# Weight transposes and scale rows of a quantised feed-forward moved from TensorE to DMA transposes and a DRAM round trip, with new instruction orders

## The chip, the cores and the metric

The kernel runs on one core of one Trainium2 chip. The metric is the device time of one execution in microseconds (us). Three runs of the kernel before stand beside each other with their median, and one more execution was taken with the profiler; all rows below are of that one. The engines are TensorE (PE; its weight loads are PEld), VectorE (DVE), ScalarE (ACT), GpSimd (POOL) and SyncE (SP), which here only issues transfers.

## The reference

One decoder layer on 8 sequences of 128 tokens with 256 features:

```
x = x + self_attention(layernorm(x))        # 16 query heads, 4 key heads, RoPE, causal, biases
x = x + cross_attention(layernorm(x), ctx)  # one head of 256, keys = values = ctx, masked
x = x + ffn(layernorm(x))
ffn: xq = quant(x); w1q = quant(w_gate_up)  # per row: scale = max|v| / 127, q = clip(round(v / scale)) * scale
     gate, up = split(xq @ w1q.T)           # 2 x 704 columns
     h = silu(gate) * up
     return quant(h) @ quant(w_down).T      # w_down is 256 x 704
```

`w_gate_up` is 1408 x 256, 11 tiles of 128 rows; its rows 704 to 1407 are the up half, that is half of tile 5 and tiles 6 to 10. Both weights come with their output rows on the partitions, so they have to be transposed before they can be multiplied, and they are quantised on the chip in each execution.

## The kernel before

Each sequence is one tile of 128 tokens. For each of the eight the kernel goes through the same steps, named by functions with the sequence's index: `project`, `rotate`, `rotate_c`, `rotate_sum`, `transpose_qk`, `evacuate_qk`, `scores`, `max_scores`, `transpose_q_max`, `score_keys`, `exp_self`, `drop_later_keys`, `weigh_values`, `normalise_y`, `project_out`, `residual_1` for self-attention; `transpose_x1`, `cross_scores`, `exp_cross`, `transpose_cross_p`, `readout`, `residual_2` for cross-attention; `quantise_x`, `transpose_x_int`, `gate_product`, `up_product`, `hidden`, `quantise_h`, `transpose_h`, `down`, `scale_down`, `add_residual` for the feed-forward.

No scheduler runs on the chip. Each engine has its own stream of instructions, and the order in it is written out by hand at the end of the engine's block (L546 to L578 for PE, L744 to L765 ACT, L1035 to L1063 DVE, L1190 to L1203 POOL). The streams meet through semaphores: `done(engine, name, j)` waits for the j-th signal. An instruction that waits holds up all that stand behind it on its engine. The sequences are interleaved, so that PE works on one while the other engines work on the next ones.

PSUM's banks tie the orders together. `ps_s` (four banks) holds the scores, and in the feed-forward the gate and up products; `gate_product(0)` therefore waits until the last `exp_self` is done. `ps_q` holds projections and their transposes, `ps_y` the attention output and later `down`, `ps_x` the cross-attention. `ps_r` is the one for everything else: the warm-up matmuls `keep_warm` (L262, matmuls of zeros at the start), `mean_ctx` (L280), `readout`, `transpose_x_int`, and all transposes of the weights. Each user of `ps_r` names the signal it has to wait for, the evacuation of the user before it.

The weights go this way. SP loads W1 in three parts and W2 in one, and the context last (L241 to L244). DVE takes the absolute maxima, the scales and their inverses; ACT writes integers, `quantise_w1(0..4)` (L638) into `w1_int`, `quantise_w2` into `w2_int`, both int16. The gate half is rescaled on POOL, transposed by PE in f32 and split into a high and a low part. The up half stays integer: PE transposes it as 16-bit data in two steps (`transpose_up`, L399, 6 transposes each), ACT evacuates it to `up_int` (`evacuate_up`, L656). Its scales, one per output column, are spread over all partitions by `spread_up_scale` (L410, 3 f32 matmuls each, which the trace shows as 6) and evacuated to `up_row` (L666); POOL multiplies the gate by that row (`widen_gate`, L1147). W2 is transposed in two halves (`transpose_w2`, L420, 6 transposes and the spread of its scale), and DVE evacuates it to `w2_T` and `w2_row` (`evacuate_w2`, L953), which `down` and `scale_down` use.

SP's queue issues the loads at the start and then waits for each output tile and stores it (L245 to L251).

Of the kernel before, what the change touches and what calls it, by code (L numbers as in the profile page):

```python
# [32 lines left out]
def decoder_layer(nc, w_first_in, x_zero_in, x_first_in, x_second_in, wo_in, mask_in, x_in, xT_in, ctxT_in, ctx_in, w1_in, w2_in, out):  # L33
# [15 lines left out]
    GT = -(-FF // P)  # L49
# [7 lines left out]
    with ExitStack() as stack:  # L57
# [46 lines left out]
        w2_row = sb("w2_row", [P, D])  # L104
# [60 lines left out]

        def x_token(j):
            return x_second[:, 0:D] if j == 1 else x_aug[:, j, 0:D]

        def x_feature(j, c):
# [30 lines left out]
            up_transposed up_int_ready up_scale_spread up_row_ready  # L200
            w2_amax_done w2_scale_done w2_inv_ready w2_int_ready w2_transposed w2_ready
# [32 lines left out]
        def _(sp):  # L234
# [10 lines left out]
            for j in range(B):  # L245
                if j < B - 1:
# [3 lines left out]
                sp.dma_start(out[j], y_out[:, j, :]).then_inc(s["out_stored"], 16)  # L250
            sp.wait_ge(s["out_stored"], 16 * B)  # L251
# [3 lines left out]
        def _(pe):  # L255
# [143 lines left out]
            def transpose_up(p, last, k):  # L399

                bank_r_free(pe, last, k)
                done(pe, "w1_int_ready", 3 + p)
                done(pe, "ident_b_ready", 0)
                for i, o in enumerate(range(5 + 3 * p, 8 + 3 * p)):
                    for c in range(DC):
                        last = nc.tensor.transpose(ps16(ps_r)[:, (2 * i + c) * P:(2 * i + c + 1) * P],
                                                   w1_int[:, o, c * P:(c + 1) * P].bitcast(BF16), ident_b[:, :])
                last.then_inc(s["up_transposed"], 1)

            def spread_up_scale(p, last, k):  # L410
# [850 lines left out]
```

## Time and profile before

| | |
|---|---|
| three runs | 102.81, 101.42, 103.0 us; median 102.81 |
| profiled execution | 101.47 us, of which the span of instructions is 99.8 |
| granted TensorE clock over the span | 0.987 of full |
| PE, PEld busy | 90.2 us (90%), 68.8 (69%) |
| DVE, ACT, POOL busy | 75.7, 65.7, 66.1 us |
| chain that ended last | PE 72%, DVE 10%, POOL 7%, issue 5%, ACT 3% |
| DMA | 8.34 MB, nearly all of it in the first 23 us |

The profile is of one execution. Busy time is per engine over the span of 99.8 us; matmuls are pipelined, and their ends are modelled, so busy times of neighbouring groups overlap by a little. The chain of waits is followed back from the last instruction, at each step to what released it or to the instruction before it on its engine; its durations don't overlap. The 1.7 us between span and execution time are start and end around the instructions.

### The profile page before, as it was taken

The numbers are of one execution on the slowest core, as the hardware profiler recorded it, in microseconds if no ns is written. First come the engines' busy times: TensorE is split into PE (matmuls) and PEld (weight loads), VectorE is DVE, ScalarE is ACT, GpSimd is POOL, SyncE is SP. The second block draws the span as 40 slices with busy tenths as digits, with TensorE's granted clock in tenths as the row PEclk, the third lists the DMA queues.
The fourth block names the chain that finished last, engine by engine and source line by source line (L and its number), as shares of the span: only waits on it lengthen the run. The fifth ranks groups of instructions, "written<-read, shape, count | busy, mean of one in ns | idle before, by whom it ended". The sixth has DMA issues, their size and how long they took to land.

```text
span 99.8 us, 2432 instructions
## 1 busy us (share of the span) xinstructions
PE 90.2 (90%) x804; PEld 68.8 (69%) x804; DVE 75.7 (76%) x217; ACT 65.7 (66%) x175; POOL 66.1 (66%) x136
## 2 busy tenths in 40 slices
PE   5999699999889999989999999979999999999560
PEld 4698467977576676767776777768778887775220
DVE  5046979957998988877896659797977788988731
ACT  1404216938839886776597878969986996988410
POOL 6266847975787977914638788848868962892220
PEclk9999999999999999999999999999999999999995
DMA  2999999940000000000000000000000010012121
GB/s 36 346 337 415 419 407 409 360 143 3 3 0 7 0 3 0 7 0 0 0 7 0 0 0 0 3 7 0 0 0 0 0 56 7 0 59 99 55 103 53
DMA packets 4521, 8.34 MB, mean 84 GB/s; under 512 B 349, under 2 KB 3358, under 8 KB 4382
## 3 DMA queue, kind: packets, MB, share of 16 engines
q1 hardware_dynamic: 4272, 7.96, 21.7%
q10 hardware_dynamic: 238, 0.23, 0.9%
q8 instruction: 6, 0.10, 0.4%
q14 instruction: 5, 0.04, 0.1%
HBM read 7.15 MB, written 1.05 MB: 82 GB/s over the span
## 4 chain that ended last, share of the span: by engine, by line
PE 72%; DVE 10%; POOL 7%; issue 5%; ACT 3%; DVEq 0%; POOLq 0%; ACTq 0%
PE ps_s L443 14%; PE ps_r L262 6%; PE ps_q L303 6%; PE ps_y L525 4%; PE ps_r L289 4%; PE ps_r L386 3%; PE ps_x L375 3%; PE ps_s L339 3%; PE ps_y L351 3%; PE ps_y L359 3%; PE ps_q L311 2%; PE ps_x L365 2%; DVE rot L846 2%; PE ps_s L469 2%; PE ps_y L354 2%
## 5 line engine op out<-in xcount | busy, mean ns | idle before, releaser
L1156 POOL TENSOR_TENSOR gate_up<-gate,up_row 128x704 f32<-128x704 f32 x7 | 11.9, 1698 | 3.7 <-ACT gate L723 3.5
L262 PE MATMUL ps_r<-warm 128*128 128x256 bf16 x60 | 9.4, 317 | 1.1 <-DVE warm L771 1.1
L262 PEld LDWEIGHTS ps_r<-warm 128*128 128x128 bf16 x60 | 6.7, 115 | 3.0 <-DVE warm L771 1.1
L1125 POOL TENSOR_TENSOR rot_c<-rot,b_rope 128x128 f32<-128x128 f32 x8 | 3.7, 459 | 7.5 <-DVE rot L846 7.5
L869 DVE RECIPROCAL y_rsum<-ps_y 128x128 f32<-128x128 f32 x8 | 7.6, 951 | 1.1 <-PE ps_y L354 1.0
L443 PE MATMUL ps_s<-gate_hi,x_int_T 128*128 128x352 f32 x28 | 7.5, 350 | 0.0
L1187 POOL TENSOR_TENSOR y_out<-ffn,x_aug 128x256 f32<-128x256 f32 x7 | 5.1, 729 | 3.7 <-DVE ffn L1025 3.7
L525 PE MATMUL ps_y<-w_T,h_T 128*128 128x256 bf16 (+1 forms) x42 | 6.5, 276 | 0.9 <-DVE ffn L1025 0.8
L443 PE MATMUL ps_s<-up_int,x_int_T 128*128 128x352 f32 x32 | 6.9, 337 | 0.0
L443 PE MATMUL ps_s<-gate_lo,x_int_T 128*128 128x352 f32 x28 | 6.8, 323 | 0.0
L610 ACT ACTIVATE p_self_T<-ps_s 128x512 f32<-128x512 f32 x8 | 4.8, 597 | 2.4 <-PE ps_s L339 2.4
L734 ACT ACTIVATE h_int<-hid,h_inv 128x704 int16<-128x704 f32 x7 | 6.1, 878 | 0.3 <-DVE h_inv L1020 0.2
L1006 DVE SCALAR_TENSOR_TENSOR hid<-ps_s,x_scale,gate_up 128x704 f32<-128x704 f32 x5 | 4.8, 951 | 1.9 <-PE ps_s L443 1.3
L1011 DVE TENSOR_REDUCE h_amax<-hid 128x1 f32<-128x704 f32 x7 | 6.1, 872 | 0.0
L525 PEld LDWEIGHTS ps_y<-w_T,h_T 128*128 128x128 bf16 (+1 forms) x42 | 3.5, 97 | 3.5 <-issue 1.5
L864 DVE TENSOR_REDUCE qk_rot<-ps_s 128x4 f32<-128x512 f32 x8 | 5.4, 678 | 0.5 <-PE ps_s L327 0.4
L723 ACT ACTIVATE gate<-ps_s,x_scale 128x704 f32<-128x704 f32 x5 | 4.2, 847 | 2.3 <-PE ps_s L443 2.3
L846 DVE TENSOR_TENSOR rot<-ps_q,rope_r 128x256 f32<-128x256 f32 x8 | 3.4, 423 | 2.9 <-PE ps_q L303 2.9
L1025 DVE SCALAR_TENSOR_TENSOR ffn<-ps_y,h_scale,w_row 128x256 f32<-128x256 f32 x8 | 3.8, 480 | 2.2 <-PE ps_y L525 1.3
L303 PE MATMUL ps_q<-wqkv_c,xT 128*128 128x192 f32 x24 | 5.4, 346 | 0.0
L375 PE MATMUL ps_x<-ctxT,x1c_T 128*128 128x128 f32 x32 | 5.3, 288 | 0.0
L386 PE MATMUL ps_r<-ctx_aug,p_cross_T 128*128 128x257 f32 x16 | 5.2, 406 | 0.0
(194 smaller groups left out, 285.8 us busy)
## 6 DMA issues: line engine op xcount, KB each, us to landing
ctxT<-in_ctxT SPq DMA_DIRECT2D x1, 1024.0 KB, 8.6
w_raw<-in_w SPq DMA_DIRECT2D x2, 512.0 KB, 11.0
ctx_aug<-in_ctx SPq DMA_DIRECT2D x1, 1024.0 KB, 17.0
out_x<-y_out SPq DMA_DIRECT2D x8, 128.0 KB, 1.7
x_aug<-in_x SPq DMA_DIRECT2D x1, 768.0 KB, 6.8
xT<-in_xT SPq DMA_DIRECT2D x1, 768.0 KB, 9.8
w_raw<-in_w SPq DMA_DIRECT2D x1, 704.0 KB, 14.6
x_first<-in_x_first SPq DMA_DIRECT2D x1, 416.0 KB, 4.3
```

The source lines that it names most:

```text
L262: nc.tensor.matmul(ps_r[:, 0:2 * T], warm[:, 0:P], warm[:, :], start=True, stop=True)
L303: last = nc.tensor.matmul(ps_q[:, 0:6 * QK], x_feature(j, c), wqkv_c[:, c, :, :], start=c == 0, stop=c == DC - 1)
L375: last = nc.tensor.matmul(ps_c, x1c_T[j % 3][:, c, :], ctxT[:, j, c, :], start=False, stop=c == DC - 1)
L386: nc.tensor.matmul(ps_r[:, 0:DA], p_cross_T[:, j, :], ctx_aug[:, j, :], start=True, stop=True).then_inc(s["readout_done"], 1)
L443: last = nc.tensor.matmul(ps_s[:, first + i, 0:FH], x_int_T[:, j, c, :], w[:, c, i * FH:(i + 1) * FH], start=c == 0 and w is parts[0], sto ...
L525: last = nc.tensor.matmul(ps_y[:, 0:D], h_T[j % 2][0:n, f, :], w2_T[0:n, f, :], start=f == 0, stop=f == FC - 1)
L734: nc.scalar.mul(h_int[j % 2][:, :], hid[j % 2][:, :, :].rearrange("p i f -> p (i f)"), h_inv[:, j:j + 1]).then_inc(s["h_int_ready"], 1)
L846: nc.vector.tensor_tensor(rot[j % 3][:, :, :].rearrange("p (m t) n -> p m (t n)", m=2), ps_q[:, 0:4 * QK].unsqueeze(1).to_broadcast([P, 2, ...
L864: nc.vector.tensor_reduce(qk_rot[j % 3][:, 0, :, DH], ps_s[:, :, 0:T], AX.X, ALU.max, negate=True).then_inc(s["negmax_done"], 1)
L869: nc.vector.reciprocal(y_rsum[j % 3][:, :], ps_ys).then_inc(s["y_rsum_done"], 1)
L1011: nc.vector.tensor_reduce(h_amax[:, j:j + 1], hid[j % 2][:, :, :].rearrange("p i f -> p (i f)"), AX.X, ALU.max, apply_absolute_value=True) ...
L1156: nc.gpsimd.tensor_tensor(gate_up[j % 2][:, :, :], gate[j % 2][:, :, :], up_row[:, :].rearrange("p (i f) -> p i f", i=2), ALU.mult).then_i ...
```

## The change

The up half of W1 and all of W2 are no longer transposed by PE. SP issues a transposing transfer from SBUF to SBUF: one for the six up tiles (twelve blocks of 128 x 128 16-bit values) as soon as `quantise_w1(4)` is done, into a region of `w1_raw`, which is free by then; and two for W2 (six blocks each), after DVE has written W2's integers as bf16 into another region of `w1_raw` padded to 768 columns (`widen_w2`). ACT then only casts the up half (`evacuate_up`, now by halves of the contraction, from SBUF). W2's transfers write `w2_T` directly.

All 13 columns of scales (11 of W1, 2 of W2) are in one tile `w_scale`. One small transpose on PE turns it into 13 rows, ACT copies them (`copy_scales`), SP stores them to DRAM, waits for that store, and loads 960 values back, broadcast to 128 partitions (`out_rows`), which takes the place of `up_row` and `w2_row`. `scale_down` and the first `widen_gate` wait for that load.

The gate half goes the way it did. The orders of all four engines are new; in the diff their parts around the moved work stand. Of removed functions only the first line is shown, since they are printed above.

```diff
-GT = -(-FF // P)
+GT = FF // P
...
-w1_scale = sb("w1_scale", [P, WT])
+w_scale = sb("w_scale", [P, WT + DC])
-w1_q = sb("w1_q", [P, GT, D])
+w1_q = sb("w1_q", [P, GT + 1, D])
-up_row = sb("up_row", [P, FF])
+scale_rows = sb("scale_rows", [WT + DC, P])
+out_rows = sb("out_rows", [P, FF + D])
-w2_scale = sb("w2_scale", [P, DC])
-w2_row = sb("w2_row", [P, D])
...
+w1_flat = w1_raw[:, :, :].rearrange("p o d -> p (o d)")
+UT = (WT - GT) * DC * P // 2
+up_T = w1_flat[:, 0:UT].bitcast(I16).rearrange("p (o c t) -> p o c t", c=DC, t=P)
+padded = w1_flat[:, UT:UT + 2 * FC * P].bitcast(BF16).rearrange("p (i f) -> p i f", f=FC * P)
+w2_bf = padded[:, 0:DC]
+h_bf = [padded[:, DC + i] for i in range(2)]
+w1_scale = w_scale[:, 0:WT]
+w2_scale = w_scale[:, WT:WT + DC]
+up_row = out_rows[:, 0:FF]
+w2_row = out_rows[:, FF:FF + D]
+scale_rows_dram = nc.dram_tensor("scale_rows_dram", [WT + DC, P], F32).ap()
...
+    done(sp, "w1_int_ready", 4)
+    sp.dma_start_transpose(up_T[:, :, :, :].rearrange("p o c t -> p (o c) t"),
+                           w1_int[:, GT:WT, :].rearrange("p o d -> p (o d)")).then_inc(s["up_T_loaded"], 16)
+    done(sp, "scale_rows_ready", 0)
+    sp.dma_start(scale_rows_dram, scale_rows[:, :]).then_inc(s["scale_rows_stored"], 16)
+    sp.wait_ge(s["scale_rows_stored"], 16)
+    sp.dma_start(out_rows[:, :], scale_rows_dram.rearrange("o p -> (o p)")[FF:2 * FF + D].unsqueeze(0).to_broadcast([P, FF + D])).then_inc(s["rows_loaded"], 16)
+    done(sp, "pads_zero", 0)
+    for c in range(DC):
+        done(sp, "w2_bf_ready", c)
+        sp.dma_start_transpose(w2_T[:, :, c * P:(c + 1) * P], w2_bf[:, c, :]).then_inc(s[f"w2_T_{c}_loaded"], 16)
+
+    def store_out(j):
+
+        if j < LAST:
             done(sp, "y_out_ready", j)
         else:
             done(sp, "last_y_out_ready", 0)
         sp.dma_start(out[j], y_out[:, j, :]).then_inc(s["out_stored"], 16)
...
-    def transpose_up(p, last, k):
...
-    def spread_up_scale(p, last, k):
...
+    def transpose_scales(last, k):
 
         bank_r_free(pe, last, k)
         done(pe, "w1_scale_done", 2)
+        done(pe, "w2_scale_done", 0)
         done(pe, "ident_ready", 0)
-        for i, o in enumerate(range(5 + 3 * p, 8 + 3 * p)):
...
+        nc.tensor.transpose(ps_r[0:WT + DC, 0:P], w_scale[:, :], ident[:, :]).then_inc(s["scales_transposed"], 1)
...
-            done(pe, "w2_ready", DC - 1)
+            for c in range(DC):
+                pe.wait_ge(s[f"w2_T_{c}_loaded"], 16)
...
-    keep_warm(30); mean_w_first(); keep_warm(6); bias_wo(); keep_warm(4); project(0); keep_warm(11)
-    transpose_qk(0); mask_scores(0); project(1); scores(0); keep_warm(7); transpose_q_max(0)
-    keep_warm(2); score_keys(0); transpose_qk(1); mean_ctx(None, 0); project(2); weigh_values(0)
-    mask_scores(1); transpose_gate(0, "valid_ready", 0); scores(1); transpose_qk(2); project_out(0)
...
-    transpose_up(0, "x_int_T_ready", 2); score_keys(7); project_out(6); cross_scores(5); gate_product(0)
-    readout(4, "up_int_ready", 0); transpose_cross_p(5); weigh_values(7); transpose_x1(6)
-    readout(5, "x2_ready", 4); cross_scores(6); transpose_up(1, "x2_ready", 5); gate_product(1)
-    up_product(0); transpose_cross_p(6); transpose_x_int(3, "up_int_ready", 1); project_out(7)
-    transpose_x1(7); up_product(1); transpose_x_int(4, "x_int_T_ready", 3); cross_scores(7)
-    readout(6, "x_int_T_ready", 4); gate_product(2); transpose_w2(0, "x2_ready", 6)
...
+    keep_warm(30); mean_w_first(); keep_warm(6); bias_wo(); keep_warm(2); mask_scores(0); project(0)
+    keep_warm(11); transpose_qk(0); scores(0); project(1); keep_warm(5); transpose_q_max(0)
+    keep_warm(4); score_keys(0); transpose_qk(1); keep_warm(3); mask_scores(1); scores(1); project(2)
+    weigh_values(0); transpose_q_max(1); mean_ctx(None, 0); score_keys(1); transpose_qk(2)
+    transpose_gate(0, "valid_ready", 0); project_out(0); project(3); mask_scores(2); scores(2)
+    transpose_x1(0); weigh_values(1); transpose_gate(1, "gate_lo_ready", 0); transpose_q_max(2)
+    transpose_qk(3); cross_scores(0); score_keys(2); project(4); project_out(1); transpose_cross_p(0)
+    transpose_gate(2, "gate_lo_ready", 1); mask_scores(3); transpose_x1(1); scores(3); transpose_qk(4)
+    weigh_values(2); transpose_scales("gate_lo_ready", 2); transpose_q_max(3); cross_scores(1)
+    score_keys(3); readout(0, "scale_rows_ready", 0); project(5); mask_scores(4); project_out(2)
...
+    cross_scores(5); project_out(6); gate_product(0); weigh_values(7); transpose_cross_p(5)
+    up_product(0); transpose_x1(6); readout(5, "x2_ready", 4); cross_scores(6); project_out(7)
+    transpose_x_int(3, "x2_ready", 5); gate_product(1); transpose_cross_p(6)
+    transpose_x_int(4, "x_int_T_ready", 3); transpose_x1(7); up_product(1); cross_scores(7)
+    readout(6, "x_int_T_ready", 4); gate_product(2); transpose_cross_p(7); readout(7, "x2_ready", 6)
+    transpose_h(0); up_product(2); transpose_x_int(5, "x2_ready", 7); gate_product(3)
...
-    def evacuate_up(p):
...
-    def evacuate_up_scale(p):
...
+    def evacuate_up(c):
+
+        act.wait_ge(s["up_T_loaded"], 16)
+        nc.scalar.copy(up_int[:, c, 0:FL], up_T[:, 0, c, FL:P])
+        nc.scalar.copy(up_int[:, c, FL:FF].rearrange("p (o t) -> p o t", t=P), up_T[:, 1:WT - GT, c, :]).then_inc(s["up_int_ready"], 1)
+
+    def copy_scales():
+
+        done(act, "scales_transposed", 0)
+        nc.scalar.copy(scale_rows[:, :], ps_r[0:WT + DC, 0:P]).then_inc(s["scale_rows_ready"], 1)
...
+    copy_key_bias(); centre_wo(); scale_v(0); evacuate_qk(0); evacuate_q_max(0); scale_v(1); exp_self(0)
+    evacuate_qk(1); quantise_w1(0); scale_v(2); quantise_w1(1); evacuate_q_max(1); quantise_w1(2)
+    quantise_w1(3); quantise_w1(4); evacuate_qk(2); exp_self(1); upper_gate(0); quantise_w2(0)
+    scale_v(3); square_1(0); quantise_w2(1); evacuate_x1(0); evacuate_q_max(2); evacuate_qk(3)
+    upper_gate(1); exp_cross(0); exp_self(2); evacuate_cross_p(0); upper_gate(2); scale_v(4)
+    square_1(1); evacuate_qk(4); evacuate_x1(1); copy_scales(); evacuate_q_max(3); evacuate_up(0)
+    exp_self(3); exp_cross(1); evacuate_up(1); evacuate_cross_p(1); square_2(0); scale_v(5); square_1(2)
...
-    def evacuate_w2(c):
...
+    def widen_w2(c):
+
+        if c == 0:
+            done(dve, "w1_int_ready", 4)
+            nc.vector.memset(padded[:, :, FF:], 0.0).then_inc(s["pads_zero"], 1)
+        done(dve, "w2_int_ready", c)
+        nc.vector.tensor_copy(w2_bf[:, c, 0:FF], w2_int[:, c, :]).then_inc(s["w2_bf_ready"], 1)
...
         done(dve, "down_done", j)
-        nc.vector.scalar_tensor_tensor(ffn[j % 3][:, :], ps_y[:, 0:D], h_scale[:, j:j + 1], w2_row[:, :],
+        dve.wait_ge(s["rows_loaded"], 16)
+        nc.vector.scalar_tensor_tensor(ffn[j % 3][:, :], ps_y[:, 0:D], h_scale[:, j:j + 1], w2_row,
                                        ALU.mult, ALU.mult).then_inc(s["ffn_ready"], 1)
...
+    stats_1(0); aggregate_1(0, 1); sum_wq(); copy_ident(); centre_w_first(); stats_1(1)
+    aggregate_1(1, 2); find_valid(); rotate(0); stats_1(2); rotate_sum(0); stats_1(3); exclude()
+    stats_1(4); stats_1(5); max_scores(0); rotate(1); stats_1(6); stats_1(7); rotate_sum(1)
+    aggregate_1(2, B); amax_w1(0); scale_w1(0); invert_w1(0); max_scores(1); rotate(2)
+    amax_w1(1); scale_w1(1); invert_w1(1); rotate_sum(2); amax_w1(2); scale_w1(2); invert_w1(2)
+    invert_sums(0); normalise_y(0); keep_valid(); amax_w2(); scale_w2(); invert_w2(); residual_1(0)
+    rotate(3); lower_gate(0); max_scores(2); rotate_sum(3); invert_sums(1); widen_w2(0)
+    negate_ctx_mean(); max_cross(0); normalise_y(1); bias_cross(0); lower_gate(1); rotate(4)
+    residual_1(1); invert_cross_sum(0); rotate_sum(4); lower_gate(2); max_scores(3); invert_sums(2)
...
+    step_x(4); invert_x(4); invert_sums(7); finish_gate(0); normalise_y(7); residual_2(5); max_cross(6)
+    amax_x(5); bias_cross(6); residual_1(7); hidden(0); amax_h(0); step_x(5); invert_x(5)
+    scale_h(0); invert_h(0); finish_gate(1); max_cross(7); invert_cross_sum(6); bias_cross(7)
+    residual_2(6); amax_x(6); invert_cross_sum(7); hidden(1); residual_2(7); step_x(6); invert_x(6)
...
-            done(pool, "up_row_ready", 1)
+            pool.wait_ge(s["rows_loaded"], 16)
...
+    rstd_1(0, 1, 1); scale_rope(0); sum_bias(); rope_bias(); rotate_c(0); rstd_1(1, 2, 2); centre_x(0)
+    scale_rope(1); rotate_c(1); centre_x(1); rstd_1(2, B, 3); drop_later_keys(0); scale_rope(2)
+    centre_x(2); scale_rope(3); rotate_c(2); centre_x(3); rescale_gate(0); scale_rope(4)
+    rescale_gate(1); scale_rope(5); centre_x(4); centre_x(5); rescale_gate(2); drop_later_keys(1)
...
```

## Rows read from the trace of the kernel before

**Rows 1.** The page: busy time and instructions by engine; granted clock in 40 slices.
```profile
PE 90.2 (90%) x804; PEld 68.8 (69%) x804; DVE 75.7 (76%) x217; ACT 65.7 (66%) x175; POOL 66.1 (66%) x136
...
PEclk9999999999999999999999999999999999999995
```

**Rows 2.** Table by stretches: width, busy us of PE, PEld, DVE, ACT, POOL; clock, DMA.
```profile
16.50:30.00 13.50, 12.68 (x135) 10.28 (x135) 11.53 (x27) 9.14 (x26) 10.97 (x23) 1.00 0.35 124
...
30.00:40.00 10.00, 9.71 (x113) 6.84 (x113) 8.96 (x26) 8.23 (x27) 7.99 (x20) 1.00 0.01 2
...
65.00:75.00 10.00, 9.41 (x68) 7.81 (x69) 8.65 (x26) 8.38 (x19) 7.29 (x12) 1.00 0.01 2
```

**Rows 3.** Chain that ended last: start, us on the chain, what.
```profile
47.75 0.67 PE ps_r L416 x6
...
49.42 0.26 PE ps_x L380
...
55.34 0.51 PE ps_r L406 x6
...
61.60 0.36 PE ps_r L406 x6
...
69.05 0.47 PE ps_r L426 x6
69.52 0.43 PE ps_r L428 x2
...
70.84 0.63 PE ps_r L426 x6
```

**Rows 4.** Timeline of PE, 65 to 71 us: start, us, line, idle before.
```profile
65.43 0.41 PE L365 MATMUL ps_x<-ident,x1c 128*128 128x128 f32 x2 [0.76 <-DVE x1c L879]
...
70.84 0.63 PE L426 MATMUL ps_r<-ident_b,w_int 128*128 128x128 bf16 x6 [0.16 <-DVE w_row L958]
```

**Rows 5.** Groups by line and shape: count, busy us, mean ns.
```profile
L956 DVE CAST w_T<-ps_r 128x640 bf16<-128x640 int16 x2 | 1.0, 492 | 0.3 <-PE ps_r L428 0.3
...
L957 DVE CAST w_T<-ps_r 64x128 bf16<-64x128 int16 x2 | 0.4, 206 | 0.0
...
L958 DVE COPY w_row<-ps_r 128x128 f32<-128x128 f32 x2 | 0.5, 273 | 0.0
...
L672 ACT COPY up_row<-ps_r 128x384 f32<-128x384 f32 x1 | 0.5, 468 | 0.0
...
L664 ACT CAST up_int<-ps_r 128x768 fp32r<-128x768 int16 x1 | 0.8, 802 | 0.1
...
L703 ACT CAST h_T<-ps_x 128x640 bf16<-128x640 int16 x4 | 2.7, 685 | 0.6 <-PE ps_x L492 0.5
...
L704 ACT CAST h_T<-ps_x 64x128 bf16<-64x128 int16 x4 | 1.0, 258 | 0.0
```

**Rows 6.** Timelines of POOL and PE around 16 us.
```profile
15.75 1.34 POOL L1089 TENSOR_TENSOR r<-ln_var,pow_exp 128x6 f32<-128x6 f32 x1
...
18.09 0.64 POOL L1130 TENSOR_SCALAR_AFFINE_SELECT p_self_T<-p_self_T 128x512 f32<-128x512 f32 x1
...
16.43 3.78 PE L289 MATMUL ps_r<-mean_w,ctxT 128*128 128x60 f32 x32
```

**Rows 7.** Timeline of ACT: last W1 quantisation; fourth query-maximum evacuation.
```profile
23.54 1.31 ACT L642 ACTIVATE w_int<-w_raw,w_inv 128x256 int16<-128x256 f32 x3
...
33.66 0.27 ACT L605 COPY q_max_T<-ps_s 128x128 f32<-128x128 f32 x1
```

**Rows 8.** The page: GB/s by slice, the two queues, the output stores.
```profile
GB/s 36 346 337 415 419 407 409 360 143 3 3 0 7 0 3 0 7 0 0 0 7 0 0 0 0 3 7 0 0 0 0 0 56 7 0 59 99 55 103 53
...
q1 hardware_dynamic: 4272, 7.96, 21.7%
q10 hardware_dynamic: 238, 0.23, 0.9%
...
out_x<-y_out SPq DMA_DIRECT2D x8, 128.0 KB, 1.7
```

More of the change, by code:

```diff
@@ L552, in _ @@
-            transpose_x1(0); transpose_qk(3); mask_scores(2); scores(2); weigh_values(1); project(4)
-            transpose_q_max(2); cross_scores(0); score_keys(2); transpose_gate(2, "gate_lo_ready", 1)
-            project_out(1); mask_scores(3); scores(3); transpose_cross_p(0); weigh_values(2); transpose_x1(1)
-            transpose_q_max(3); transpose_qk(4); readout(0, "gate_lo_ready", 2); score_keys(3); project(5)
-            cross_scores(1); mask_scores(4); project_out(2); scores(4); transpose_qk(5); transpose_cross_p(1)
@@ L557, in _ @@
-            weigh_values(3); transpose_q_max(4); readout(1, "x2_ready", 0); transpose_x1(2); score_keys(4)
-            project(6); cross_scores(2); mask_scores(5); transpose_x_int(0, "x2_ready", 1); project_out(3)
-            scores(5); transpose_qk(6); transpose_cross_p(2); transpose_x_int(1, "x_int_T_ready", 0)
-            weigh_values(4); transpose_q_max(5); project(7); transpose_x1(3); score_keys(5)
-            readout(2, "x_int_T_ready", 1); cross_scores(3); mask_scores(6); project_out(4)
@@ new lines, in _ @@
+            weigh_values(2); transpose_scales("gate_lo_ready", 2); transpose_q_max(3); cross_scores(1)
+            score_keys(3); readout(0, "scale_rows_ready", 0); project(5); mask_scores(4); project_out(2)
+            transpose_cross_p(1); scores(4); transpose_x1(2); weigh_values(3); readout(1, "x2_ready", 0)
+            transpose_q_max(4); transpose_qk(5); cross_scores(2); score_keys(4)
+            transpose_x_int(0, "x2_ready", 1); project_out(3); project(6); mask_scores(5); transpose_cross_p(2)
@@ new lines, in _ @@
+            scores(5); transpose_x1(3); weigh_values(4); transpose_q_max(5); readout(2, "x_int_T_ready", 0)
+            transpose_qk(6); score_keys(5); cross_scores(3); transpose_x_int(1, "x2_ready", 2); project(7)
+            project_out(4); mask_scores(6); transpose_cross_p(3); scores(6); weigh_values(5); transpose_x1(4)
+            transpose_q_max(6); transpose_qk(7); readout(3, "x_int_T_ready", 1); score_keys(6); cross_scores(4)
+            project_out(5); mask_scores(7); transpose_x_int(2, "x2_ready", 3); scores(7); transpose_cross_p(4)
@@ L581, in _ @@
+            transpose_h(4); last_gate(0); down(3); last_gate(1); up_product(7); transpose_h(5); down(4)
+            transpose_h(6); down(5); down(6); last_transpose_h_a(); last_transpose_h_b(); last_down_a()
+            last_down_b()
         @block.scalar
```

170 lines of the change are left out of this document (53 added, 117 removed).

## The prediction

> **What bounds the kernel now.** I read the page's busy times first. TensorE (PE) is busy 90.2 of 99.8 us, the other three between 65 and 76, and the granted clock is full in every slice but the last [rows 1]; so neither the clock nor a single slow stage is to be looked for, and the question is whether PE's own work is the path. The table by stretches says so: from 30 to 40 us PE is busy 9.71 of 10 us, as much in the ten that follow, and from 65 to 75 it is 9.4, while VectorE (DVE) has 8.96 in the first of these stretches and ScalarE (ACT) 8.2 [rows 2]. The chain of waits then goes from PE group to PE group through the whole middle, and among its pieces stand all the transposes and spreads that the change takes away, each with the time that it holds on the chain [rows 3]. PE's timeline shows where it does stand still late in the kernel: 0.76 us before `transpose_x1(7)`, for a residual of DVE, and 0.16 us between the two W2 transposes [rows 4].
>
> **Taken from PE.** Two `spread_up_scale` at 0.67 us each, two `transpose_up` at 0.51 and 0.36, and for W2 0.47 and 0.63 for the transposes and twice 0.43 for the spread of its scale (of each pair of spreads one stands) [rows 3]: 1.34 + 0.87 + 1.96 = 4.17 us. The 0.16 us wait between the W2 halves goes too, because nothing of W2 passes through the shared bank `ps_r` any more [rows 4]: 4.33.
>
> **Added to PE.** One f32 transpose of 13 columns. The nearest row is a whole 128-column f32 transpose with 0.26 us of chain [rows 3]; it can't cost more, and not less than nothing. I take 0.2. The count of warm-up matmuls goes from 60 to 61, all ahead of the 16 us mark, where PE waits anyway: nothing. What hides it is the wait for loads and rotations; uncovered it would be one matmul of that kind.
>
> **DVE.** `evacuate_w2` goes: per half 0.49 + 0.21 + 0.27 us [rows 5], 1.94 in all, at 70 to 73 us, when PE has other work; worth nothing beyond the 0.16 counted. `widen_w2` comes: two int16 to bf16 copies of 704 columns and a memset of 4 x 64 columns. The nearest copy is 640 columns out of PSUM in 0.49 [rows 5]; from SBUF it may be twice as fast, so a copy costs 0.27 to 0.54 and both with the memset 0.6 to 1.3; I take 1.0, nearer the row. They fall between about 28 and 36 us, where DVE has only 1.04 us in 10 free [rows 2]. About a third should show: 0.3.
>
> **ACT.** Removed: the scale rows (0.47 for the larger, about 0.4 for its pair) and the up evacuations (0.80 for the second, and about as much for the first, of 640 columns in two pieces) [rows 5], about 2.5 us. Added: per half of up a cast of 640 columns and one of 64, by the h casts 0.69 and 0.26 [rows 5], so 1.9, and the 0.26 copy of the scales. The sum hardly changes, but 1.9 us move from 57 to 63 us to about 34 to 38 us, in front of `exp_self(3)` and `exp_cross(1)`. The two W2 quantisations leave that stretch for the one before, where ACT is busy 9.1 of 13.5 us [rows 2]; that is the cover. With four small fillers taken out of PE's order as well, some handover in between that was hidden by them is now seen. None of it has a row; bounds are 0 and the 1.9 us, and as the loops through the banks are much shorter than the five us per sequence, I take 0.4.
>
> **The start.** `scores(0)` now comes before `project(1)`, which brings the first sequence forward, and `mean_ctx` comes after `weigh_values(0)` and `transpose_q_max(1)`. `mean_ctx` used to cover a wait: its 3.78 us ran from 16.43 us on while GpSimd (POOL) took 1.34 us for the power of six columns from 15.75 us and masked the probabilities only at 18.09 [rows 6]. Now the mask follows the power directly, 17.1 + 0.64 = 17.7 us. PE gets there after `scores(1)` and `project(2)` at about 17.1, so it idles some 0.6 us, then does the same work as before. Against that, scores and rotation are further on. Counting the same set of PE pieces done, I come to a loss between 0.1 and 0.7 and take 0.2.
>
> **The late gap.** In the new order `normalise_y(7)` and `project_out(7)` stand ahead of `hidden(0)`'s work, so the 0.76 us before `transpose_x1(7)` may go wholly or not at all; I take 0.4.
>
> **SP's queue and the transfers.** What is queued behind SP's new waits: the row store and load, the two W2 transposes, and only then the output stores. The first store is due near 79 us, so none of them is held up unless the whole queue is some 40 us late. Of the new transfers three have much room: the scale rows are needed by `widen_gate(0)` at 60 us and written near 34, and a 128 KB output store lands 1.7 us after its issue [rows 8], so store and a broadcast of 492 KB are over near 39; the W2 transposes are needed by `down(0)` near 73. They cost nothing.
>
> The up transpose is the one that can hurt. `quantise_w1(4)` runs from 23.5 to 24.9 us now and moves forward, so 24.9 is the latest issue; `evacuate_up(0)` stands directly behind `evacuate_q_max(3)`, which now runs at 33.66 [rows 7]. The room is 9.0 us, and behind the waiting ACT instruction stand `exp_self(3)` and everything after it, so each us beyond goes straight onto the end. No row shows a transposing transfer. Lower bound: its 393 KB at the 410 GB/s of the load phase are 1.0 us, with the 1.7 of landing 2.7. As 1,536 pieces of 256 bytes, by the ACT queue's packets (0.9% of 16 x 99.8 us over 238 packets, 60 ns each) 1,536 x 60 / 16 = 5.8 us, with landing 7.5; by the SP queue's mean of 81 ns 9.5 [rows 8]. Upper bound: twelve blocks of 128 x 128 one after the other, each at a whole small transfer's 1.7 us, 20.4. I take 7.5, since small packets are the nearest row: in time, by 1.5 us, cost 0.
>
> Two pages of the Trainium skill disagree on this transfer. "DMA: Bandwidth & Descriptors", section "Latency and other measured facts", has a DMA transpose at 261 GB/s with a broken middle dimension; by that the up half would take an estimated 1.5 us and the sum stays. "VectorE: DVE Perf Modes", section "The three transpose paths", gives 1309 ns for one 128 x 128 block and advises TensorE for it; twelve in a row would be an estimated 15.7 us, 6.7 late, and the kernel would be near 104.6 us. No row here tells which holds.
>
> **Sum.** -4.33 + 0.2 + 0.3 + 0.4 + 0.2 - 0.4 = -3.6 us. The profiled execution took 101.47 us for its span of 99.8, so it would become 97.9, with a span near 96.2. The median of the three runs, 102.81, is 1.3 above the profiled one; from there the same gain leads to 99.2. I take 98.6, between the two.
>
> **Rivals.**
> A, the forecast: PE stays the bound and the removed work is gained. For it: the chain pieces [rows 3] and the full stretches [rows 2]. Its own range is 96.6 to 100.4. Chance 0.64.
> B, the removed pieces were fillers. DVE at 8.96 in 30 to 40 us takes 1.0 more, ACT gets 1.9 in front of `exp_self(3)`, and PE waits for them instead. If all of it shows, 1.3 + 1.9 in place of my 0.7, and the late gap stays as well, the gain is 3.6 - 2.5 - 0.4 = 0.7 us; so 100.8 to 102.1, middle 101.4. Against it: PE stands idle for only a few tenths in those stretches. Chance 0.20.
> C, slower: the up transpose lands late and ACT stands at `evacuate_up(0)`. It decides from 9.0 us on, that is from 0.75 us per block; 3.6 beyond that and the gain is eaten, 5.7 beyond it and the kernel is slower by over 2%. At 1.7 us per block it is 11.4 late: 101.47 - 3.6 + 11.4 = 109.3. For it: no row excludes serial blocks, and the room by the nearest row is only 1.5 us. Against: the loads keep 16 engines busy at once. Chance 0.16, of which 0.02 falls within 2%.
>
> **Numbers.** About 2% is what a measurement of this kernel can tell from no change; 2% of 102.81 is 2.06, so faster is below 100.75. A gives 0.63 faster and 0.01 same, B 0.03 faster and 0.17 same, C 0.14 slower and 0.02 same: 0.66, 0.20, 0.14. The range 96.6 to 102.9 leaves out C's slower part and about 0.05 below.
>
> **What would show it.** In the profile after: no instructions on the old transpose and spread lines; PE still over 90% busy with a span near 96; ACT's first up cast begins without an idle time put down to a DMA, and the transfer's time from issue to landing is under 9 us; DVE's W2 copies at 0.3 to 0.5 us; PE idle near 17 us of about 0.6 before `weigh_values(0)`; the 0.76 us gap before `transpose_x1(7)` smaller. What would prove me wrong: an idle time of several us on ACT before the up cast (C), or PE's idle time between 20 and 75 us grown by 2 to 3 us with DVE or ACT as releaser (B).

## The result and the profile after

The changed kernel takes 97.93 us in the median of 4 runs (97.44 to 98.35), where the kernel before took 102.12 beside it (4 runs, 101.11 to 103.0). The ratio is 0.967, with a 95% interval of 0.960 to 0.974. Sent again with the last experiments it has a ratio of 0.964 (0.960 to 0.969); two of those 6 runs, 98.94 and 98.98 us, were in a slower state with a lower granted clock (0.974 and 0.975), and here as below medians, ranges and ratios leave such runs out (median of the other four 97.94). The forecast was 98.6; the sum of its terms gave 97.9 and a span of 96.2, and the span is 95.7.

The busy times of the page, its granted clock in 40 slices and the chain by engine, of the kernel after:

```profile
PE 86.5 (90%) x766; PEld 66.0 (69%) x766; DVE 74.8 (78%) x214; ACT 64.5 (67%) x175; POOL 66.2 (69%) x136
...
PEclk9999999999999999999999999999999999999995
...
PE 50%; DVE 23%; POOL 11%; issue 7%; ACT 5%; DVEq 0%; POOLq 0%; ACTq 0%
```

PE has lost 3.7 us of work, its share is the same 90% as in [rows 1], and the clock is full as before. But the chain is on PE for 50% of the span only, where it was 72%. From 18 to 32 us it now runs over DVE, with two short pieces of POOL (start, us on the chain):

```profile
18.90 1.14 DVE w_amax L920
...
28.89 0.14 DVE w_raw L959
```

The second line is the memset of `widen_w2(0)`, which the change has put in. From 40.5 to 50 us most of the chain is on POOL (5.4 us). The table by stretches, with the columns of [rows 2]:

```profile
16.50:30.00 13.50, 12.64 (x132) 10.37 (x129) 12.28 (x33) 10.14 (x26) 11.09 (x23) 1.00 0.52 155
...
30.00:40.00 10.00, 9.86 (x110) 7.35 (x112) 9.41 (x27) 8.68 (x31) 7.79 (x16) 1.00 0.41 85
...
65.00:75.00 10.00, 9.49 (x63) 7.71 (x62) 8.04 (x21) 9.19 (x20) 9.05 (x13) 1.00 0.00 0
```

Against [rows 2] PE is as full as it was, and DVE is fuller: 12.28 of 13.5 us in the first stretch (11.53 before) and 9.41 of 10 in the second (8.96). PE and DVE are now nearly equally busy up to 40 us, and as the chain shows, PE is not the engine that sets the time everywhere.

Where along the kernel the time came is read from the starts of the same PE work. PE's timeline of the kernel before: the first projection, the first of the two pieces of `gate_product(0)`, and the first of `last_gate(0)`.

```profile
8.65 0.65 PE L303 MATMUL ps_q<-wqkv_c,x_first 128*128 128x192 f32 x3
...
57.22 0.57 PE L443 MATMUL ps_s<-gate_hi,x_int_T 128*128 128x352 f32 x2
...
86.25 0.43 PE L469 MATMUL ps_s<-gate_hi,x_int_T 128*128 128x352 f32 x1
```

PE's timeline of the kernel after, the same three and the waits of which the prediction spoke:

```profile
8.64 0.55 PE L336 MATMUL ps_q<-wqkv_c,x_first 128*128 128x192 f32 x2
...
18.12 0.43 PE L384 MATMUL ps_y<-p_self_T,v_pad 128*32 128x128 f32 x8 [0.74 <-POOL p_self_T L1133]
...
55.52 0.59 PE L453 MATMUL ps_s<-gate_hi,x_int_T 128*128 128x352 f32 x2
...
62.38 0.44 PE L398 MATMUL ps_x<-ident,x1c 128*128 128x128 f32 x2 [0.24 <-ACT p_cross_T L640]
...
66.77 0.67 PE L419 MATMUL ps_r<-ctx_aug,p_cross_T 128*128 128x257 f32 x2 [0.45 <-ACT p_cross_T L640]
...
82.36 0.43 PE L479 MATMUL ps_s<-gate_hi,x_int_T 128*128 128x352 f32 x1
```

The first projection starts at the same time in both. `gate_product(0)` is 1.70 us earlier and `last_gate(0)` 3.89, so the gain was made in two parts. Below, "the distance to last_gate(0)" is its start minus that of the first projection: 77.60 us before, 73.72 after. It leaves out by how much a profiled execution started late (up to 1.1 us between executions of these kernels) and the end.

SP's queue (start, us held, what) and ACT's up casts of the kernel after:

```profile
23.69 1.52 SPq L257 DMA_TRANSPOSE w_raw<-w_int  x1
33.85 0.40 SPq L260 DMA_DIRECT2D scale_rows_dram<-scale_rows  x1
...
35.66 2.63 SPq L266 DMA_TRANSPOSE w_T<-w_raw  x2
```

```profile
34.03 0.25 ACT L668 CAST up_int<-w_raw 128x64 fp32r<-128x64 int16 x1
34.17 0.73 ACT L669 CAST up_int<-w_raw 128x640 fp32r<-128x640 int16 x1
```

The up transpose is issued at 23.69, 10.3 us ahead of the cast, holds SP for 1.52 us, and the page has it landed after 3.7. No idle time stands before the cast.

### The profile page after: what moved, and what is told of

It reads as the page before. It is cut to its first block, busy times and chain, and to the rows that moved or that the text cites. A ratio compares the mean times of both kernels' runs of the same rounds, so it can differ in the third digit from the quotient of the medians.

```text
span 95.7 us, 2358 instructions
## 1 busy us (share of the span) xinstructions
PE 86.5 (90%) x766; PEld 66.0 (69%) x766; DVE 74.8 (78%) x214; ACT 64.5 (67%) x175; POOL 66.2 (69%) x136
## 4 chain that ended last, share of the span: by engine, by line
PE 50%; DVE 23%; POOL 11%; issue 7%; ACT 5%; DVEq 0%; POOLq 0%; ACTq 0%
PE ps_s L453 14%; PE ps_r L295 6%; PE ps_y L535 4%; PE ps_r L419 3%; DVE qk_rot L858 3%; PE ps_q L336 2%; DVE rot L848 2%; PE ps_x L408 2%; DVE w_amax L920 2%; PE ps_s L372 2%; POOL rot_c L1128 2%; DVE y_rsum L871 2%; PE ps_s L479 2%; DVE w_amax L945 2%; PE ps_q L502 2%
## 5 line engine op out<-in xcount | busy, mean ns | idle before, releaser
L1159 POOL TENSOR_TENSOR gate_up<-gate,out_rows 128x704 f32<-128x704 f32 x7 | 11.9, 1703 | 2.9 <-ACT gate L725 1.7
L1133 POOL TENSOR_SCALAR_AFFINE_SELECT p_self_T<-p_self_T 128x512 f32<-128x512 f32 x8 | 5.1, 642 | 2.5 <-ACT p_self_T L619 2.5
L651 ACT ACTIVATE w_int<-w_raw,w_inv 128x256 int16<-128x256 f32 x11 | 4.8, 498 | 1.5 <-DVE w_inv L931 1.4
L453 PEld LDWEIGHTS ps_s<-up_int,x_int_T 128*128 128x128 f32 x32 | 5.2, 190 | 0.1
L453 PEld LDWEIGHTS ps_s<-gate_hi,x_int_T 128*128 128x128 f32 x28 | 4.5, 188 | 1.1 <-DVE gate L966 0.5
## 6 DMA issues: line engine op xcount, KB each, us to landing
xT<-in_xT SPq DMA_DIRECT2D x1, 768.0 KB, 10.3
```

The costliest lines, as they stand in the source:

```text
L453: last = nc.tensor.matmul(ps_s[:, first + i, 0:FH], x_int_T[:, j, c, :], w[:, c, i * FH:(i + 1) * FH], start=c == 0 and w is parts[0], sto ...
L1133: nc.gpsimd.affine_select(out=p_self_T[j % 3][:, :, :], in_=p_self_T[j % 3][:, :, :], compare_op=ALU.is_ge, fill=0.0, base=0, pattern=[[0, ...
L1159: nc.gpsimd.tensor_tensor(gate_up[j % 2][:, :, :], gate[j % 2][:, :, :], up_row.rearrange("p (i f) -> p i f", i=2), ALU.mult).then_inc(s[" ...
```

## The experiments

**1. The transposes moved, the orders left.** The changed kernel with PE's, ACT's, DVE's and POOL's orders as they were before; only the removed calls are missing and the new ones are put in.

```
 PE, old order:  - spread_up_scale(0); spread_up_scale(1); transpose_up(0); transpose_up(1)
                 - transpose_w2(0); transpose_w2(1)
                 + transpose_scales("gate_lo_ready", 2)   before transpose_q_max(3)
 ACT:            - evacuate_up_scale(0), (1)    + copy_scales() after quantise_w2(1)
 DVE:            - evacuate_w2(0), (1)          + widen_w2(0), (1) after residual_1(2)
```

> The transfers and the DRAM round trip as in the changed kernel, but the old orders of all four engines; only the small scale transpose, its copy and the two bf16 copies are put in, and the up casts stand at their old late places. Theory (removed work is the gain): 97.5 to 99.0 us, about 4 below the kernel before, within 1 of the changed kernel. Rival (the orders are the gain): 101 us or more.

Measured: 102.11 us (9 runs, 101.2 to 102.6), 101.3 for the kernel before; ratio 1.007 (1.003 to 1.011), as the rival had it. The removal with what it needs gains nothing in the old orders. PE is busy 87.2 us, so the work is gone. PE's timeline shows the scale transpose that was added, `readout(6)`, and waits that are new:

```profile
8.22 0.82 PE L336 MATMUL ps_q<-wqkv_c,x_first 128*128 128x192 f32 x4
...
33.26 0.28 PE L438 MATMUL ps_r<-ident,w_scale 128*13 128x128 f32 x1 [0.23 <-DVE gate_lo L933]
...
39.34 0.33 PE L366 MATMUL ps_s<-ident,qk_rot 128*128 128x128 f32 x1 [0.40 <-DVE qk_rot L861]
...
49.10 0.43 PE L384 MATMUL ps_y<-p_self_T,v_pad 128*32 128x128 f32 x8 [0.41 <-POOL p_self_T L1125]
...
67.09 0.70 PE L419 MATMUL ps_r<-ctx_aug,p_cross_T 128*128 128x257 f32 x2
...
69.75 0.91 PE L453 MATMUL ps_s<-up_int,x_int_T 128*128 128x352 f32 x4 [0.56 <-DVE hid L1003]
...
71.38 0.59 PE L453 MATMUL ps_s<-gate_hi,x_int_T 128*128 128x352 f32 x2 [0.72 <-ACT gate L722]
...
85.98 0.43 PE L479 MATMUL ps_s<-gate_hi,x_int_T 128*128 128x352 f32 x1
```

None of these five waits stands in the kernel before. They are put down to three different engines, and the distance to last_gate(0) is 77.76 us, 0.16 more than before. For comparison PE's timeline of the kernel before, the matmul that stands at 39.34 above and `readout(6)`:

```profile
38.68 0.33 PE L333 MATMUL ps_s<-ident,qk_rot 128*128 128x128 f32 x1
...
67.07 0.70 PE L386 MATMUL ps_r<-ctx_aug,p_cross_T 128*128 128x257 f32 x2
```

Counted from the first projection, experiment 1 is 1.09 us late at the first of these, and that is still ahead of the first removed piece (47.6 us in the kernel before). Nearly all of this loss comes from what was added: 0.51 us are lost at the scale transpose, which waits 0.23 us for DVE, and 0.47 at the wait of 0.40 us, where DVE does both copies of `widen_w2` and their memset (38.07 to 38.7 us) just ahead of the maximum that PE needs. From there the removal does gain something: at `readout(6)` the kernel is only 0.45 us late, at last_gate(0) 0.16. So of the 2.21 us of pieces taken away up to `readout(6)` at most 0.64 us is gained, and of W2's 2.12 us 0.29. The last two waits lie where the W2 transposes were: in the kernel before PE did them at 69.05 to 71.5 us [rows 3], while ACT loaded a table (1.28 us) and computed the silu. They were fillers. ACT's timeline of experiment 1:

```profile
69.19 1.28 ACT L722 ACT_TABLE_LOAD   x1 [0.24 <-PE ps_s L453]
```

**2. The orders moved, the transposes left.** The old PE transposes and spreads, put by hand into the new orders.

```
 PE, new order:  - transpose_scales(...)
                 + spread_up_scale(0) after project_out(4), (1) after cross_scores(4)
                 + transpose_up(0) after transpose_x1(5), (1) after project_out(6)
                 + transpose_w2(0) after up_product(2), (1) after gate_product(3)
```

> All weight transposes and scale spreads back on TensorE, as in the kernel before, but in the new orders of all four engines; the pieces are put where the shared bank is free nearest to their old places. Theory (the gain is TensorE's removed work, 4.2 us of chain pieces): the execution is back at about 101 to 102.5 us, no better than the kernel before. Rival (the new orders are the gain): it stays near 98 to 99 us.

Measured: 106.77 us (3 runs, 105.96 to 107.04), ratio 1.049 (1.041 to 1.058): worse than either kernel, and both expectations missed. PE's timeline:

```profile
56.23 0.70 PE L386 MATMUL ps_r<-ctx_aug,p_cross_T 128*128 128x257 f32 x2 [0.72 <-ACT up_int L661]
...
75.76 0.28 PE L434 MATMUL ps_r<-ident_b,x_int 128*128 128x128 bf16 x2 [0.91 <-DVE w_row L955]
...
77.01 0.27 PE L434 MATMUL ps_r<-ident_b,x_int 128*128 128x128 bf16 x2 [0.96 <-ACT x_int L691]
```

The stretch from 75 to 80 us in the table, same kernel:

```profile
75.00:80.00 5.00, 2.82 (x13) 1.72 (x14) 2.23 (x6) 3.69 (x8) 1.54 (x2) 0.75 0.00 0
```

The first two of these waits are for evacuations of `ps_r`, the bank that the old pieces share with `readout` and `transpose_x_int`; the third is for ACT's x_int. After the waits at 76 us the clock is granted at 0.75 over the stretch. My placing is surely not the best; the run shows that these pieces don't fit into the new orders at places chosen by eye, not that none would do. Experiments 1 and 2 together: neither half of the change gives the gain, as far as the new orders were tried without the other half.

**3 and 4. Is PE the bound?** 38 warm-up matmuls (256 columns each) were put in at six places between 50 and 72 us, in the changed kernel and in the kernel of experiment 1. On the chain they hold 4.20 us (6, 6, 5, 3, 9 and 9 of them at 0.66, 0.66, 0.55, 0.33, 1.00 and 1.00), about what the change removed.

```
 + fill(6) before readout(3); fill(6) before transpose_x_int(2); fill(5) before readout(4)
 + fill(3) before readout(5); fill(9) after gate_product(2);     fill(9) after up_product(2)
```

> The changed kernel with 38 warm-up matmuls put into TensorE's order where the removed pieces stood (6, 6, 5 and 3 in the attention part, 9 and 9 after gate_product(2) and up_product(2)), about 4.2 us of TensorE work that nobody reads. Nothing else waits for them. Theory revised after the first four runs (the new orders have used up the room in which the old pieces lay, so TensorE is the bound in them): 3 to 4.2 us longer than the changed kernel, 101 to 102 us. Rival (TensorE's work is hidden in these orders too, and the gain comes from the removed evacuations and bank waits): under 1.5 us longer.

> The same 38 matmuls at the same places in the kernel with the old orders and the transfers. Theory (in the old orders the removed pieces lay in the shadow of other waits: evacuations, the Silu table load, residuals): at most 1.5 us longer than without them, 102.2 to 103.7 us. Rival (TensorE bounds there too): 3 to 4.2 us longer, 105.5 us or more.

Measured: the changed kernel with fillers 101.23 us (10 runs), ratio 0.995 (0.991 to 0.999), against 0.967 (0.960 to 0.974) without; old orders with fillers 103.97, ratio 1.023 (1.016 to 1.030), against 1.007 (1.003 to 1.011). The first is as expected; the second lies just above its range (102.2 to 103.7) and far below the rival's. First projection, `readout(6)` and last_gate(0), PE's timeline of the changed kernel with fillers:

```profile
9.66 0.54 PE L341 MATMUL ps_q<-wqkv_c,x_first 128*128 128x192 f32 x2
...
66.67 0.60 PE L424 MATMUL ps_r<-ctx_aug,p_cross_T 128*128 128x257 f32 x2
...
86.97 0.43 PE L484 MATMUL ps_s<-gate_hi,x_int_T 128*128 128x352 f32 x1
```

Of the changed kernel, the same `readout(6)` in the first profile, and first projection and last_gate(0) run again:

```profile
63.96 0.60 PE L419 MATMUL ps_r<-ctx_aug,p_cross_T 128*128 128x257 f32 x2
```

```profile
9.68 0.54 PE L336 MATMUL ps_q<-wqkv_c,x_first 128*128 128x192 f32 x2
...
83.40 0.43 PE L479 MATMUL ps_s<-gate_hi,x_int_T 128*128 128x352 f32 x1
```

Of the old orders with fillers:

```profile
8.50 0.82 PE L341 MATMUL ps_q<-wqkv_c,x_first 128*128 128x192 f32 x4
...
69.19 0.70 PE L424 MATMUL ps_r<-ctx_aug,p_cross_T 128*128 128x257 f32 x2
...
88.25 0.43 PE L484 MATMUL ps_s<-gate_hi,x_int_T 128*128 128x352 f32 x1
```

The distances are 77.31 against 73.72, so the fillers cost 3.59 us in the new orders; in the old ones 79.75 against 77.76, 1.99 us. In the new orders 85% of the added PE work goes onto the end, in the old ones 47%. `readout(6)` shows where the two differ, because 20 of the fillers stand ahead of it and the last 18 behind it. Up to it the fillers cost 1.69 us in the new orders and 1.82 in the old ones, much the same. The last 18, 2.00 us on the chain, stand where W2's pieces were: they cost 1.90 us in the new orders and 0.17 in the old ones. So the room that the new orders have used up is the one around W2's pieces. The test says what added work costs, not what removed work gains: in the old orders at most 0.64 us was gained up to `readout(6)` when 2.21 were taken out, and the fillers cost 1.82. For one thing they do not stand at the same places: the first six come behind the wait of 0.41 us for POOL at 49.10, and `spread_up_scale(0)` had stood ahead of it. One of the longer pieces, from the chain of waits of the changed kernel with fillers (start, us on the chain):

```profile
68.84 1.00 PE ps_r L295 x9
```

**5 and 6. The up transpose late.** In 5 the `DMA_TRANSPOSE` of up is issued behind those of W2, at 38.7 us; in 6 ACT's two casts are moved behind `square_2(2)` and `square_2(3)` as well.

```
 SP:   - done(sp, "w1_int_ready", 4); sp.dma_start_transpose(up_T, w1_int[:, GT:WT, :]) ...
         (scale rows, W2 transposes)
       + the same two lines here
 ACT (6 alone):  evacuate_up(0) from behind evacuate_q_max(3) to behind square_2(2)
                 evacuate_up(1) from behind exp_cross(1)      to behind square_2(3)
```

> The changed kernel with one edit: SP issues the up transpose last, after the scale rows and the two W2 transposes, so near 38.5 us in place of 23.7. With 3.7 us from issue to landing it lands near 42.5, while ScalarE wants to cast at 34.0. Theory (ScalarE stands in order and everything hangs behind the cast, each us late is a us on the end): ScalarE idle about 8 us before the first up cast, the execution 7 to 9 us longer, 105 to 107 us. Rival (slack on ScalarE and in the later stages takes up a part): 2 to 5 us longer.

> The late transfer of the run before, but with ScalarE's two up casts moved behind square_2(2) and square_2(3), near 47 and 51 us. Theory (only the place of the casts set the deadline; the transfer itself is hidden): within 0.7 us of the changed kernel, 97.3 to 98.6 us. Rival (the casts in their early place filled free time of ScalarE and now push the attention steps): 1 to 2 us longer than the changed kernel.

Measured: 5 takes 108.64 us (108.14 to 109.38), ratio 1.070 (1.063 to 1.077); 6 takes 98.57 (98.45 to 99.04), ratio 0.971 (0.966 to 0.977), within what its theory had. In 5, ACT's timeline, PE's, and the table at three places:

```profile
42.75 0.24 ACT L668 CAST up_int<-w_raw 128x64 fp32r<-128x64 int16 x1 [8.40 <-DMA w_raw<-w_int]
```

```profile
44.17 0.61 PE L355 MATMUL ps_s<-causal,ident_b 128*128 128x128 bf16 x4 [7.90 <-ACT p_self_T L619]
```

```profile
40.00:44.00 4.00, 0.00 (x0) 0.00 (x0) 0.00 (x0) 1.25 (x3) 0.00 (x0) 0.50 0.59 114
...
48.00:49.00 1.00, 1.00 (x10) 0.65 (x3) 0.52 (x1) 0.14 (x1) 0.18 (x1) 0.50 0.00 0
...
50.00:51.00 1.00, 1.00 (x15) 0.76 (x13) 0.57 (x3) 0.84 (x4) 0.00 (x0) 1.00 0.00 0
```

ACT stands 8.40 us for the transfer, PE 7.90 for ACT, and the distance to last_gate(0) is 84.20 us, 10.48 more than in the changed kernel. That is more than the 7 to 9 us expected. The other 2.6 us are the clock: PE's first work after the idle time is granted 0.50 (1.2 of 2.4 GHz), still so at 49 us, and full again only at 50. The delay against the changed kernel is 8.0 us at 44.17 and 10.46 at 49.9, and stays there to last_gate(0), so all of the 2.5 us are lost in the stretch at half the clock. In 6 the same late transfer costs 0.6 us of distance (74.32). So the room of this transfer is a matter of where the cast stands in ACT's order.

**7 and 8. Twelve transposes in place of one.** In 7 the up half is transposed by 12 instructions of one 128 x 128 block each, cast where it was; in 8 SP also waits for each to land before it issues the next, and the casts are at the late places of experiment 6.

```
 for n in range(12):
     sp.dma_start_transpose(up_T_blocks[:, n:n+1, :], w1_int_up[:, n*128:(n+1)*128]).then_inc(up_T_loaded, 16)
     (8 alone)  sp.wait_ge(up_T_loaded, 16 * (n + 1))
```

> The up half as twelve transposing transfers of one 128 x 128 block, issued one behind the other without waits. In the changed kernel one instruction took 1.5 us to issue and 3.7 to land. Theory (the transfer is paid by its pieces, in parallel on the queue's engines): issue 12 x 0.4 to 0.6, all landed 6 to 8 us after the first issue, no wait on ScalarE, time like the changed kernel's. Rival C of the prediction (blocks are moved one after another at 1 us or more): landed 14 us or more after the first issue, ScalarE waits.

> The same twelve transfers, each issued only when the one before has landed, with the up casts late as in up_late_cast_late, so that the wait does not decide the time. It measures what one dependent transposing block costs: by the output stores (1.7 us from issue to landing) 12 x 1.9 = 23 us. If a single block took as long as the whole half (3.7 us) it would be 45 us and the scale rows and W2 would come late for widen_gate(0) and down(0).

Measured, one run each: 107.15 us and 106.58. SP's queue of 7 and ACT's first up cast:

```profile
23.80 16.12 SPq L258 DMA_TRANSPOSE w_raw<-w_int  x12
```

```profile
41.06 0.24 ACT L669 CAST up_int<-w_raw 128x64 fp32r<-128x64 int16 x1 [6.81 <-DMA w_raw<-w_int]
```

SP's queue of 8 and its first up cast:

```profile
24.45 28.30 SPq L258 DMA_TRANSPOSE w_raw<-w_int  x12
```

```profile
53.87 0.24 ACT L670 CAST up_int<-w_raw 128x64 fp32r<-128x64 int16 x1 [5.62 <-DMA w_raw<-w_int]
```

16.12 us over 12 is 1.34 us for an instruction of one block, while one instruction of twelve blocks takes 1.52. So the cost sits in the issue, by instruction and hardly by size: 7 is slow because SP is still issuing until 39.9 us. With a wait in between, a block costs 28.30 / 12 = 2.36 us, not the 1.9 expected, so the late casts of 8 are not late enough: ACT stands 5.62 us, PE 6.11, the distance is 82.07 us, 8.35 more than in the changed kernel, and the clock is 0.50 from 55 to 61 us. In 7 ACT stands 6.81 us, PE 6.32, and the distance grows by 9.55 us to 83.27: again some 3 us more than the wait, at a clock of 0.50 from 42 to 49 us. 7 is the prediction's third case, made real by a small edit.

The Trainium skill, "VectorE: DVE Perf Modes", section "The three transpose paths", gives 1309 ns for a block by DMA; the 1.34 us for which an instruction with one block holds the queue is near it, the 2.3 us to its landing are not, and the 1.52 us for twelve shows that it must not be multiplied by the blocks of one instruction. "DMA: Bandwidth & Descriptors", section "Latency and other measured facts", has 261 GB/s, an estimated 1.5 us for 393 KB; the trace shows 1.52 us at the queue and 3.7 to the landing, so the estimate is near the first and well under the second.

**9 to 12. Can more be had in the same way?** The changed kernel again, with two edits, alone and together, all on one chip. `mean_split` puts `mean_ctx`'s first sequence into the 0.74 us before `weigh_values(0)`. `x_int_dma` transposes the x_int of sequences 0 to 2 by SP's queue.

```
 mean_split:  project(2); + mean_ctx(0, 1); weigh_values(0); transpose_q_max(1); mean_ctx(1, B)
 x_int_dma:   PE - transpose_x_int(0), (1), (2);  ACT evacuate_x_int(j) -> cast_x_int(j), j < 3
              SP + sp.dma_start_transpose(x_int_D[:, j], x_int[:, j]), j < 3, behind W2's
```

> The changed kernel once more, on the chip and beside the runs of the three kernels sent with it, so that they can be compared with it: 97.4 to 98.4 us, ratio 0.96 to 0.972 to the kernel before. Both theories give this.

> The first of mean_ctx's eight sequences (with its start, some 0.5 us of PE) is computed before weigh_values(0), where PE waits 0.74 us for POOL's mask in the changed kernel. Theory (in the new orders PE's time decides to the end, idle time at the start too): 0.3 to 0.6 us less than the changed kernel, 97.3 to 97.7 where that one has 97.9. Rival (the start is bound by DVE's and POOL's chain, 12.28 us of DVE busy in the 13.5 us from 16.5 to 30, and PE's idle time there is free): no change, 97.8 to 98.1.

> The x_int of sequences 0 to 2 are transposed by the DMA queue of SP too (3 more DMA_TRANSPOSE, two 128x128 blocks each), and PE's 3 transpose pairs, 0.22 us each, are gone; ScalarE casts from the landed copy instead of from PSUM. Theory (PE is the bound between 35 and 60 us): 0.4 to 0.7 us less, 97.2 to 97.5. Rival (an instruction DMA_TRANSPOSE takes 1.35 us to issue and lands some 2.5 us after its start, and ScalarE stands in front of its cast as in the kernels with separate blocks): each late landing is paid in full, 98.5 to 101. A third, middle result (97.8 to 98.1) says that those PE pieces were fillers.

> Both edits, the split mean_ctx and the three x_int transposes by DMA. Theory: the gains add, 0.7 to 1.3 us less than the changed kernel, 96.6 to 97.2. Rival: the worse of the two alone decides, 98 or more.

Measured, medians and ratios to the kernel before: the changed kernel 97.94 (4 runs), 0.964 (0.960 to 0.969); `mean_split` 97.62 (6 runs), 0.962 (0.959 to 0.966); `x_int_dma` 97.37 (4 runs), 0.960 (0.956 to 0.964); both 97.22 (6 runs), 0.959 (0.955 to 0.963). The medians fall, but the intervals overlap; that the last version is faster than the changed kernel is not shown. The medians of the single edits lie where their theories had them, and the one of both just above; the traces below say that next to nothing has changed. There is little to be had: the distance to last_gate(0) is 73.72 in the changed kernel, 73.66 with the split, 73.75 with x_int by DMA, 73.63 with both. PE's timeline of `mean_split`:

```profile
24.27 0.66 PE L429 MATMUL ps_r<-ident,w_q 128*128 128x128 f32 x4 [0.65 <-DVE valid_mean L831]
```

The 0.74 us wait has gone, and 0.65 stand now 5.5 us further on, before `transpose_gate(0)`, for DVE. That fits the chain, which runs over DVE there. PE's timeline of `x_int_dma`:

```profile
48.18 0.33 PE L417 MATMUL ps_x<-ident,p_cross 128*128 128x128 f32 x1 [0.44 <-ACT p_cross L636]
...
53.39 0.33 PE L417 MATMUL ps_x<-ident,p_cross 128*128 128x128 f32 x1 [0.23 <-ACT p_cross L636]
```

The first of these waits was 0.28 us and the second is not in the changed kernel: 0.39 of the 0.66 us taken from PE show as waits for ACT, and nothing arrives at the end. So also in the new orders these pieces were fillers.

## Why the prediction was right, and which step was not

**Right in the sum.** The forecast (case A) was a median of 98.6 and 97.9 by its sum; 97.93 was measured. The order of the parts holds too: up to `gate_product(0)` the net PE work removed is 1.34 + 0.51 - 0.28 = 1.57 us, and that start came 1.70 earlier; at `last_gate(0)` it is 3.89, where the sum says 3.6. That the total came out is in part luck: it rests on new orders that the sum priced at a few tenths, and no step says why they should turn the removed work into time.

**Wrong in its reason.** "PE stays the bound and the removed work is gained" is not what the kernel before allowed. In the old orders the removal with what it needs gains nothing (1.007): 1.09 us are lost to the added scale transpose and DVE copies, and of the removed work only 0.93 us is gained. The pieces stood on the chain [rows 3] because PE did them, not because the end hung on their full length; without them the chain goes at nearly the same speed over DVE, POOL and ACT. That is near the prediction's case B, with waits for three engines where it had named extra load on two. What it took as evidence, PE 9.7 of 10 us busy [rows 2], can't tell a bound from a filled shadow. The new orders make the difference: experiment 1 and the changed kernel differ in the orders alone, and 4.04 us of distance lie between them. They give PE other needed work at those places (`readout(7)`, `transpose_h(0)` and `up_product(2)` during ACT's table load and silu, for one); the fillers show it for W2's pieces, 1.90 of 2.00 us against 0.17. I gave the orders a few tenths in both directions; they carry the whole gain, given the removal. Nor is PE the bound throughout in the changed kernel: its chain is on DVE from 18 to 32 us, and 0.66 us of PE work taken out in `x_int_dma` gained nothing. How the 4.04 us are made up piece by piece, and whether the new orders would gain with the old pieces better placed than in experiment 2, stays open.

**The terms.**
The scale transpose takes 0.28 us of PE, I took 0.2 and said that it could not be more than 0.26; in the old orders it cost 0.51 with its wait for DVE.
DVE's copies for W2 take 0.27 and 0.57 us and the memset 0.17, 1.01 in all, I took 1.0. Of these 0.34 stand on the chain of the changed kernel, where I had 0.3; in the old orders they cost 0.47.
At the start PE idles 0.74 us before `weigh_values(0)`, I took 0.6; moving work in there gave next to nothing (73.66 against 73.72), so this wait is free; what the new start costs or gains as a whole no run shows.
The 0.76 us before `transpose_x1(7)` [rows 4] are 0.24 now, but 0.45 stand before `readout(7)`: the gap moved for the most part, I had counted 0.4 as gained.
ACT's 0.4 us for the moved casts can't be read from one row. Experiment 6 is the nearest: casts moved later, with a later transfer, cost 0.6.
SP's new waits cost nothing, as argued: the W2 transposes are issued at 35.66 and land 4.2 us later, some 30 us before `down(0)`.

**The up transpose.** 3.7 us from issue to landing, where 7.5 was taken and 2.7 to 20.4 were the bounds; the room was 10.3 us in place of 9.0. The small packets do not cost what the ACT queue's packets of [rows 8] made me think. The upper bound was near: with twelve instructions the transfer lands 17.3 us after its start. What decides is that it is one instruction, and no step of mine saw that.

**Case C's price.** I had counted each late us as one. It is 10.48 for 8.40 us late (7.90 of idle PE) and 9.55 for 6.81 (6.32), because of the clock after it.

## What to carry to other kernels

A busy share of 97% in a stretch and a place on the chain do not show that an engine's work is the bound: where an order written by hand is dense, its cheap pieces may be filling other engines' latencies. Before costing a removal at its full duration, ask of each piece which wait would stand in its place; the test that tells is to remove it in the old order, and to follow the same pieces in both traces from the start, because what the removal adds elsewhere may eat what it gains. Fillers tell what more work would cost at their places, which is another number. Removing work and reordering are one change: each alone, as tried here, gave nothing or a loss, together 3.3%. A transpose by DMA should, by these runs, be one instruction over many blocks, issued early, and the engine that takes it up should have that wait late in its order.

## What the runs showed of the hardware that I had not expected

A `DMA_TRANSPOSE` holds SP's queue for 1.34 us with one block of 128 x 128 16-bit elements and for 1.52 with twelve; it lands 2.3 us after its issue with one block and 3.7 with twelve (4.1 and 5.0 in experiments 5 and 6). PE's granted clock fell from full to 0.50 in an idle time of 7.90 us and stayed there for the next 5 to 6 us of work (44.2 to between 49 and 50) before it rose; after an idle time of 6.32 us it was 0.50 too, for some 7 us (42.5 to between 49 and 50). The same DVE copy of 704 columns took 0.27 us at 28.96 and 0.57 at 34.90; POOL stood idle beside the first and worked on `rope_r` (34.79, 0.48 us) beside the second, but whether that slowed it was not tried.
